# Another order for the opening of a two-layer graph network kernel

## The reference

```
h = relu(layernorm(x))                                  # x: 1250 x 512, 40000 edges
e = concat([h[src], h[dst], edge_attr])                 # 1088 wide
m = mish(mish(e @ W1 + b1) @ W2 + b2)                   # one row of 512 for each edge
agg = segment_sum(m, dst)
u = mish(concat([h, agg]) @ W3 + b3);  y = h + u @ W4 + b4
x = x + layernorm(y) * gamma + beta
h = relu(layernorm(x))
s = (h @ U * sv) @ Vt
x = x + relu(segment_sum(s[src] * w, dst) + bias)
```

## Time and profile before

| | us |
|---|---|
| median of 3 runs (lowest, highest) | 1528.53 (1527.34, 1529.81) |
| the profiled execution, its own time | 1528.69 |
| its span | 1527.0 |
| PE busy | 1490.7 (98%) |
| DVE busy | 1417.4 (93%) |
| ACT busy | 1296.3 (85%) |
| POOL busy | 1080.8 (71%) |

### The profile page before, as it was taken

How to read it: one execution, slowest core, us unless ns; L and a number is a source line. 1 busy time by engine, 2 the same in 40 slices (tenths; PEclk the granted TensorE clock), 3 DMA queues, 4 the chain that set the end, 5 groups by cost and what they waited for, 6 DMA issues and landing times.

```text
span 1527.0 us, 33370 instructions
## 1 busy us (share of the span) xinstructions
PE 1490.7 (98%) x7862; PEld 1168.3 (77%) x7862; DVE 1417.4 (93%) x2925; ACT 1296.3 (85%) x2505; POOL 1080.8 (71%) x984
## 2 busy tenths in 40 slices
PE   7979999999999999999999999999999999999898
PEld 5767777777777777777777777777777777776785
DVE  7789999999999999999999999999999999996576
ACT  4079999999999999999999999999999999996362
POOL 2257788788788788877888878887887888762320
PEclk9999999999999999999999999999999999999999
DMA  8964555455455545545545555554544555454573
GB/s 313 314 195 115 118 124 123 115 129 116 115 125 123 119 117 124 119 117 124 121 117 121 125 121 116 125 119 116 130 117 117 121 122 124 114 136 124 124 167 151
DMA packets 122452, 205.10 MB, mean 134 GB/s; under 512 B 31641, under 2 KB 54297, under 8 KB 122416
## 3 DMA queue, kind: packets, MB, share of 16 engines
q0 software_dynamic: 59392, 116.85, 35.1%
q1 hardware_dynamic: 62672, 87.30, 18.3%
q10 hardware_dynamic: 352, 0.52, 0.1%
HBM read 151.60 MB, written 42.75 MB: 127 GB/s over the span
## 4 chain that ended last, share of the span: by engine, by line
PE 78%; issue 5%; DVE 5%; DMA 4%; POOL 4%; ACT 1%; POOLq 1%; DVEq 0%; SPq 0%; ACTq 0%
PE bm L1081 48%; PE bp L1060 6%; PE bp L1068 5%; PE bs L1104 4%; PE bp L1070 4%; PE pm L1092 2%; PE po L2047 2%; DMA agg_tab<-ev 1%; DMA xg<-A_tab,idx 1%; PE pm L1091 1%; POOL hTl L985 1%; PE pu L2025 1%; PE pu L337 1%; POOL M_tab L1010 1%; POOL agg_tab L999 1%
## 5 line engine op out<-in xcount | busy, mean ns | idle before, releaser
L985 POOL TENSOR_TENSOR hTl<-tp,hTh 128x512 fp32r<-128x512 f32 (+1 forms) x314 | 411.0, 1309 | 218.0 <-DVE khl L1270 202.5
L1081 PE MATMUL bm<-W2h,hTh 128*128 128x512 f32 x1252 | 497.9, 398 | 1.6 <-POOL hTl L985 1.0
L1081 PE MATMUL bm<-W2l,hTh 128*128 128x512 f32 x1252 | 496.9, 397 | 0.0
L1081 PE MATMUL bm<-W2h,hTl 128*128 128x512 f32 x1252 | 494.2, 395 | 0.0
L974 POOL DMA_INDIRECT xg<-A_tab,idx x305 | 319.3, 1047 | 48.8 <-issue 40.0
L1081 PEld LDWEIGHTS bm<-W2h,hTh 128*128 128x128 f32 x1252 | 235.2, 188 | 71.5 <-DVE bm L1263 14.8
L1081 PEld LDWEIGHTS bm<-W2l,hTh 128*128 128x128 f32 x1252 | 235.3, 188 | 57.2
L1081 PEld LDWEIGHTS bm<-W2h,hTl 128*128 128x128 f32 x1252 | 235.3, 188 | 52.9
L1140 ACT ACTIVATE rp<-bp 128x512 f32<-128x512 f32 (+1 forms) x314 | 183.2, 584 | 105.0 <-PE bp L1070 102.6
L1234 DVE SCALAR_TENSOR_TENSOR rp<-rp 128x512 f32<-128x512 f32 (+1 forms) x314 | 215.5, 687 | 30.0 <-ACT rp L1140 17.1
L1244 DVE SCALAR_TENSOR_TENSOR tp<-rp,bp 128x512 f32<-128x512 f32 (+1 forms) x314 | 211.3, 673 | 4.7 <-ACT rp L1146 2.4
(11 more groups left out here) (247 smaller groups left out, 2318.0 us busy)
## 6 DMA issues: line engine op xcount, KB each, us to landing
ea<-in_eaT SPq DMA_DIRECT2D x156, 128.0 KB
M_tab<-mev POOLq DMA_DIRECT2D x157, 80.0 KB
agg_tab<-ev POOLq DMA_DIRECT2D x157, 64.0 KB
db<-in_dst_rows SPq DMA_DIRECT2D x78, 128.0 KB
M<-M SPq DMA_DIRECT2D x76, 128.0 KB
xg<-A_tab,idx POOLq DMA_INDIRECT x313
eaW<-Bh_tab SPq DMA_DIRECT2D x77, 64.0 KB
eaW<-Bl_tab SPq DMA_DIRECT2D x77, 64.0 KB
```

Of the source, the lines that this page charges most:

```text
L985: e.tensor_tensor(hTl[p][:, j, 0:w], pick(u, start_t, tp)[:, 0:w], hTh[p][:, j, 0:w], ALU.subtract)\
L1081: last = e.matmul(bank[0:r, :], a[p][:, c, j * P:j * P + r], w[:, c, :], start=False, stop=c == KC - 1 and w is W2l, skip_group_check=True)
```

## The change

PE forms A1 ahead of T2 and A4 ahead of T5, where a new batch begins (FRESH). ACT's program is written out by hand: it takes over the high parts of W1's second half and of W2 (c_w1h, c_w2h), and its stores of A go to other places. On DVE the first instructions of a batch's statistics are cut off as `row_stats`, the scales move behind the next nTl, and the table `between` is dealt anew. SP issues W1's second half right behind dcoli. POOL's zeros each wait for two more transposed chunks, and three instead of two of them come after the gathers, at B products 3, 5 and 7.

```
+            FRESH = [c0 for c0, _ in BATCH[1:]]
...
+                def w1_hi():
+                    e.wait_ge(q_w1[0], 16)
+                    link(e.tensor_copy(w1h[:, 0:KC, :], w1raw[:, 0:KC, :]))
+                def w1_lo(i):
+                    k = slice(i * KC, (i + 1) * KC)
+                    if i:
+                        e.wait_ge(c_w1h, 1)
...
-                between = {0: [lambda: variances(1), lambda: scales(1)], 1: [lambda: variances(2)], 2: [windows],
...
+                between = {0: [lambda: row_stats(1), lambda: variances(1)], 1: [lambda: scales(1), lambda: row_stats(2)],
+                           2: [lambda: variances(2)], 3: [lambda: scales(2), windows], 4: [iotas],
+                           5: [lambda: w1_lo(1)], 6: [we_hi], 7: [columns], 8: [w2_lo], 9: [bases]}
...
-                    e.wait_ge(c_tr, i + 1)
+                    e.wait_ge(c_tr, i + 3)
                     zero_agg(e, i)
-                for i in range(M_EARLY - 2):
-                    e.wait_ge(c_tr, ZERO_DMAS + i + 1)
+                for i in range(M_EARLY - 3):
+                    e.wait_ge(c_tr, ZERO_DMAS + i + 3)
                     zero_m(e, i, q_z)
...
-                for i in range(M_EARLY - 2, M_EARLY):
-                    e.wait_ge(c_B, 3 * (i + 3 - M_EARLY) + 1)
+                for i in range(M_EARLY - 3, M_EARLY):
+                    e.wait_ge(c_B, 2 * (i + 3 - M_EARLY) + 3)
                     zero_m(e, i, q_z)
...
+                def w1_hi():
+                    e.wait_ge(q_w1[1], 16)
+                    e.activation(w1h[:, KC:2 * KC, :], w1raw[:, KC:2 * KC, :], ACT.Copy, scale=1.0).then_inc(c_w1h, 1)
+                def w2_hi():
+                    e.wait_ge(q_w2, 3 * 16)
+                    e.activation(W2h[:], W2raw[:], ACT.Copy, scale=-1.0).then_inc(c_w2h, 1)
...
                 for c in range(NCH):
+                    if c in FRESH:
+                        table_a(c - 1)
                     e.wait_ge(c_hT, c + 1)
...
-                    if c >= 1:
+                    if c >= 1 and c not in FRESH:
                         table_a(c - 1)
...
                 e.dma_start(dcoli[:], dst_cols).then_inc(q_dst, 16)
+                w1_half(1)
...
-                    if c == 0:
-                        w1_half(1)
```

More of the change, by code:

```diff
@@ L441, in gnn_two_layers @@
             c_pad = sem("c_pad")
+            c_w1h = sem("c_w1h")
+            c_w2h = sem("c_w2h")
+            FRESH = [c0 for c0, _ in BATCH[1:]]
             v = {}
@@ L497, in variances @@
                         c_v.inc(e.bn_stats(stats[:, c, :], xs[:, c, :]))
+                def variances(i):
+                    c0, c1 = BATCH[i]
                     later()
@@ L649, in _, with roots, relu @@
                 e.preload_act_table_set("natural_log_exp_and_others")
-                for c in range(NCH):
-                    for i in range(len(BATCH)):
[L652 to L659, removed]
+                def roots(i):
+                    c0, c1 = BATCH[i]
+                    e.wait_ge(c_v.sem, v["var", i])
+                    e.activation(lnv[:, c0:c1], var[:, c0:c1], ACT.Ln).then_inc(c_a, 1)
+                    e.wait_ge(c_a, 2 * i + 1)
+                    e.activation(rstd[:, c0:c1], lnv[:, c0:c1], ACT.Exp, scale=-0.5).then_inc(c_a, 1)
+                def relu(c):
+                    for i in range(len(BATCH)):
+                        if c == BATCH[i][0]:
                             e.wait_ge(c_v.sem, v["rstd", i])
@@ L662, in _ @@
                                  scale=rstd[:, c:c + 1]).then_inc(c_hT, 1)
[L663 to L666, removed]
+                def w1_hi():
[4 more added lines that the diff above has]
+                    e.activation(W2h[:], W2raw[:], ACT.Copy, scale=-1.0).then_inc(c_w2h, 1)
+                roots(0)
+                relu(0)
+                relu(1)
+                evac(e, 0)
+                evac(e, 1)
+                roots(1)
+                relu(2)
+                store_a(e, 0)
+                relu(3)
+                evac(e, 2)
+                store_a(e, 1)
+                relu(4)
+                evac(e, 3)
+                roots(2)
+                store_a(e, 2)
+                evac(e, 4)
+                relu(5)
+                relu(6)
+                store_a(e, 3)
+                w1_hi()
+                for c in (7, 8, 9):
+                    relu(c)
+                    evac(e, c - 2)
+                    store_a(e, c - 3)
+                w2_hi()
+                evac(e, 8)
+                store_a(e, 7)
+                evac(e, 9)
+                store_a(e, 8)
+                store_a(e, 9)
             @prologue.on("tensor")
@@ L674, in table @@
                     n = 0
-                    for a, w, part in ((nTh, w1h, "w1h"), (nTl, w1h, None), (nTh, w1l, "w1l")):
-                        if part and c == 0:
-                            e.wait_ge(c_v.sem, v[part, half])
+                    for a, w in ((nTh, w1h), (nTl, w1h), (nTh, w1l)):
+                        if c == 0 and a is nTh and w is w1h:
+                            e.wait_ge(*((c_w1h, 1) if half else (c_v.sem, v["w1h"])))
+                        if c == 0 and w is w1l:
+                            e.wait_ge(c_v.sem, v["w1l", half])
                         if half == 0 and a is nTl:
```

19 lines of the change are left out of this document (6 added, 13 removed).

## The result

The changed kernel is slower. Its median is 1533.89 us (1532.42 to 1535.99, 7 runs); the kernel before, timed beside it, 1528.70 (1527.34 to 1530.04, 7 runs). The ratio is 1.0036 (95% interval 1.0027 to 1.0046): 5.2 us more, against a forecast of 2.7 us less. The profiled execution took 1533.54 with a span of 1531.9 (before 1528.69 and 1527.0), so the profiles show 4.9 of it.

A forecast was written before the change was run, and what follows sets the result against it. PE bounds the edge loop; between the B products and it, DMA round trips, DVE and POOL do. Gain 3.7 - 0.4 (wcol) - 0.6 (zeros) = 2.7 us off 1528.69 gives 1526.0, as median 1525.8; range 1523.3 to 1530.0.

The forecast's parts named there:

- A products in front of transposes: PE before the B products: filling waits of 4.6 us, less new small waits, starts B0 3.7 us earlier as middle.
- Two small waits: New PE waits among the A products: 0.6 us together around T3, A2 and its nTl, and 0.5 before A5.
- High parts on ACT: Two copies of 2048 elements a partition on ACT, 1.7 us each (bound 3.2); cost 0 to 1.8, taken as 0.
- That wait is empty: On ACT, relus of 7 to 9 queue behind the wait for W1's load, issued early enough to cost nothing.
- wcol: Load that columns on DVE needs by 35.6: issued near 29.9, landing by 36.7 with the old 6.8; loss taken 0.4 us.
- Below nothing, above one old row: Bounds on wcol's stall: nothing if it lands below 35.6, 1.1 us with the old 6.8 from issue to landing.
- the zeros: POOL's zeros start two chunks later and one moves behind the gathers; loss in the B stores' chain taken as 0.6 us.
- the third zero: One 640 KB transfer moved behind the gathers: 1.8 us lost if served in issue order, nothing if queues take turns.
- Whatever is won ahead of it comes out of the total whole: The edge loop, PE busy 1360.1 of 1370.0 us, neither gives nor takes, so gains before it pass whole.
- the first rival: B stores' landings, not PE, set the first square at 80.26; only 0.8 us remain, total 1527.7; chance 0.20.
- The slower rival: Three B buffers: store round trips beyond 16.6 us together make the kernel slower, 1.7 us, 1530.2; chance 0.14.
- the signs listed: Expected T2 near 17.2, ACT copy 1.7, wcol's cast near 35.6, B0 near 44.5, first square near 77.5; wrong: B0 past 46.

The follow-up runs named there:

- x1: Changed kernel with columns, which waits for wcol on DVE, moved from behind chunk 7 to behind the last nTl; 1531.95 us, ratio 1.0020 to the kernel before.
- x4: Changed kernel with the loads of scoli and wcol issued right behind W1's second half, not behind A4's store; 1530.66 us, ratio 1.0010 to the kernel before.
- x2: Changed kernel with POOL's zeros as in the kernel before, in pace and in number behind the gathers; 1532.65 us, ratio 1.0026 to the kernel before.
- p2: Changed kernel with W1's second-half load and the zeros put back as before, leaving the order of work alone; 1531.24 us, ratio 1.0019 to the kernel before.
- x3: Changed kernel with two zeros behind the gathers instead of three, the pace ahead of them kept; 1533.48 us, ratio 1.0038 to the kernel before.
- b1: Kernel before with SP's four late zeros split, two behind the last B store, two behind the second group's rows; 1531.34 us, ratio 1.0017.
- p1: Kernel before with only W1's second-half load behind the destination rows and the zeros as changed; 1528.97 us, ratio 1.0002.
- x5: x4 with the three zeros behind the gathers taken out of the prologue, SP issuing seven later instead of four; 1530.37 us, ratio 1.0012 to the kernel before.

## Why the prediction was wrong

*A products in front of transposes: right.* B0 without the wait for wcol was forecast between 44.1 and 44.5; x1 has 44.30 and x4 44.94. Two small waits came as 0.25 each where 0.6 and 0.5 were forecast; the second group of A0 took 1.85 us instead of 1.47. x4 lies 0.4 outside the forecast and the reading still stands.

*High parts on ACT: right.* 1.90 and 1.91 us each, where 1.7 was taken within bounds of 1.7 to 3.2; no engine waited for them in the changed kernel. The timeline of ACT:

```profile
25.83 1.90 ACT L676 ACTIVATE w1h<-w1l_raw 128x2048 fp32r<-128x2048 f32 x1
...
36.03 1.91 ACT L681 ACTIVATE W2h<-W2l_raw 128x2048 fp32r<-128x2048 f32 x1
```

"That wait is empty" was right of the changed kernel only; x2 and p2 show what it costs (3.23 and 2.81) when the load is late.

*wcol: the step that failed.* It was put as a landing by 36.7 and "a stall of 1.1" at most, "I take 0.4". The stall was some 5.0 us, and the groups behind it ran another 1.3 slower: from the group that waited to B0 it is 51.11 - 44.90 = 6.21 in after and 44.94 - 40.05 = 4.89 in x4. Together 6.3 instead of 0.4, which turns a B0 of 44.8 into 51.1 (in x3, the same program up to T9, 3.26 and 49.11). The issue came at 31.92 instead of 29.9: the A store ahead of it was issued at 29.69 and took 0.95, and the load of scoli, which the prediction doesn't name, 1.20. But the issue is the smaller part. The step that failed is "with the old 6.8 it lands at 36.7": an old time from issue to landing set behind a new issue. The profiles have these landings:

| | before | b1 | after | x1 | x2 | x3 | p1 | p2 |
|---|---|---|---|---|---|---|---|---|
| wcol issued | 36.07 | 36.13 | 31.92 | 33.82 | 35.88 | 31.39 | 33.21 | 34.95 |
| to its landing | 6.8 | 7.1 | 9.7 | 7.0 | 5.7 | 8.7 | 6.8 | 5.5 |

Issued anywhere between 31.4 and 36.1, it landed between 40.0 and 43.2: an issue 4 us earlier brought the landing 1.2 forward. Only with its issue moved ahead of the full stretch (14.37 in x4) was it there when the changed kernel wants it. In these profiles, then, the landing hardly follows the issue, which points to the DMA work standing ahead of it, and the added 3 us are for the most part the earlier issue itself. Which of the transfers ahead count (in after two zeros are issued together at 28.83, and three more at 33.00, 36.23 and 39.45 while it is under way) wasn't measured; p1 has the new pace of zeros and 6.8. "Below nothing, above one old row" was no bound from both sides. I had also left the clock out of the price of a wait.

*Between B0 and the first edge product: 0.6 for the zeros, measured 3.0.* The stretch grew from 29.72 to 32.73. The sum had a term for the third zero and none for two others: that all zeros start two chunks later, which it names and puts at nothing without a reason, and ACT's queue. x3 speaks against the third zero, x2 has the stretch as before with the old pace. The longer issue on ACT's queue is 2.2 us of the 3.0 by the profile of after, and it is there with either pace; what makes it long stays open, and no run takes it away. How the 3.0 divide between it and the zeros' pace is not shown.

*"Whatever is won ahead of it comes out of the total whole": wrong between B0 and the loop.* I had made room for it as the first rival (landings keep the gain, 0.20) with 0.8 of a gain left. x4, where wcol is in time, comes nearest to that rival's case; it came out not at 0.8 faster but at 1.0010 (0.9999 to 1.0021). There the rival was right in kind: of PE's 3.1 us 0.9 are left when ACT's issue begins, and that issue takes them and more. x5 bears the mechanism out from its other side, by less work ahead of the landing.

*The slower rival* named the round trips of B's stores. They grew little, if at all (DVE's tb waited for Bl_tab by 0.78, 1.32 and 0.36 after, by 0.93, 0.63, 0.86 and 0.52 before; the chain has 7.02 and 3.94 after, 6.66 and 6.21 before), and nowhere near 16.6 together. The B products of after run through: PE was not slowed by the three buffers, but by the last store, the issue and the load behind it. Only where B0 comes earlier, in x1, p1 and x4, does PE wait behind the last B product for DVE's tb (3.52, 1.34, 0.71). The side was right for another reason.

Of the signs listed, T2 at 17.73 and the ACT rows fit; the cast of wcol at 41.69, B0 "later than 46", and the first square at 85.73 instead of 77.5 were those that would make it wrong, and did.

## What to carry to other kernels

Before moving an instruction that waits for a load ahead of one that PE needs, ask what stands ahead of that load on the DMA engines. Where they are full, an old time from issue to landing may not be set behind a new issue: here the load landed at 40 to 43 whenever it was issued, and issuing it before the full stretch was the cure. Where the engines are near full up to a point, PE's head start ahead of it is worth little (0.9 of 3.1 us in x4). Share times length adds up what they did, but look for idle time that a late issue made, and read the queues of all issuing engines, not only the one that was changed. Taking transfers out paid here (5.7 us at the first edge product), and it lasted only when they were not put in one piece ahead of the next gather.

## What was not expected of the hardware

- The granted clock falls after a wait of some us and comes back some us after work begins. After the 4.82 us of idle in after it is 0.50 of full (so 1.2 GHz) from 46 to 48, and from 83.84 to 85.00, after 3.03 us of idle, it is 0.50 again and products of 128x512 take 0.63 us, where x4 has 0.39 from 97.4 to 98.4 at a clock of 1.00. It doesn't do so each time: behind 3.26 us in x3 the first group took 1.20, behind 3.23 in x2 2.07.
- An issue of a DMA can hold its queue for long: 2.63 us on ACT in after, 3.90 in x4, for a transfer whose issue took 0.41 before. Full engines don't explain it: their share during the issue was 0.53 in after, 0.42 in x1 (2.16 us), 0.92 in x4, and 1.07 before, where it was short. It goes with ACT's new program in all thirteen kernels; why, no run shows.
- A transfer of 158 KB took 6.8 us from issue to landing before, and 9.75 after, with the DMA engines at 1.04 and 1.03; over eight kernels it took 5.5 to 9.7 us and landed within 3.2 us of the same time; a gather took 3.43 before and 6.44 in x5, with the engines at 0.98.
